# Six base tiles in place of five between the expert products of a two-layer adapter and expert kernel, with the tables and the first products reordered

## The reference

```python
def reference(x, id0, id1, W0, rw0, rb0, A0, B0, W1, base_w, base_b, A1, B1, rw1):
    # layer 0: one of 16 matrices (64 x 64) for each batch, over its tokens; 8 experts of rank 16, the best two
    y = einsum('bct,bcd->bdt', x, W0[id0])
    logits = y @ rw0.T + rb0
    w = gates of the two largest softmax values, normed to 1
    x = x + einsum('no,eor->..', (y @ A0) * w, B0) * 0.5
    # layer 1: one of 14 adapters (1024 x 1024) for each batch; then a base product and 16 experts of rank 64
    y = einsum('bij,bkj->bik', x, W1[id1])
    base = y @ base_w.T + base_b
    hidden = y @ A1.T
    top two of softmax(y @ rw1.T), normed
    return x + base + 0.5 * sum over the two experts of gate * hidden @ B1[e].T
```

## Time and profile before

| | |
|---|---|
| time, 3 runs | 1112.93, 1116.61 (median), 1119.01 us |
| the profiled execution | 1121.12 us, of which its span is 1119.5 us |
| PE busy | 1078.9 us, 96% of the span |
| DVE, ACT, POOL busy | 60%, 45%, 20% |
| granted clock of PE, mean | 0.985 |
| moved by DMA | 283.57 MB, 253 GB/s over the span |

### The profile page before, as it was taken

How to read it: one execution, slowest core, us unless ns; L and a number is a source line. 1 busy time by engine, 2 the same in 40 slices (tenths; PEclk the granted TensorE clock), 3 DMA queues, 4 the chain that set the end, 5 groups by cost and what they waited for, 6 DMA issues and landing times.

```text
span 1119.5 us, 21551 instructions
## 1 busy us (share of the span) xinstructions
PE 1078.9 (96%) x5804; PEld 918.8 (82%) x5805; DVE 673.3 (60%) x1230; ACT 501.0 (45%) x1021; POOL 221.2 (20%) x354
## 2 busy tenths in 40 slices
PE   5999889999999999999999999999999999999998
PEld 5999878888887888888888877877777888888887
DVE  4778743664837557564546688445555376667666
ACT  1121123654737456564536642145555344444444
POOL 1121010110202011110101000155554232222220
PEclk9999989999999999999999999799999999999999
DMA  9588582673957648583666442169999899999996
GB/s 300 192 319 318 209 318 99 229 271 118 340 183 231 245 138 327 192 271 119 235 229 233 94 135 93 60 228 342 351 352 354 335 407 366 336 363 331 319 342 207
DMA packets 126125, 283.57 MB, mean 253 GB/s; under 512 B 28146, under 2 KB 35570, under 8 KB 124146
## 3 DMA queue, kind: packets, MB, share of 16 engines
q1 hardware_dynamic: 96592, 180.59, 45.5%
q0 software_dynamic: 29216, 102.25, 25.9%
q10 hardware_dynamic: 258, 0.01, 0.0%
HBM read 181.50 MB, written 101.29 MB: 253 GB/s over the span
## 4 chain that ended last, share of the span: by engine, by line
PE 80%; DVE 6%; DMA 5%; ACT 3%; issue 3%; SPq 2%; ACTq 0%; POOL 0%; DVEq 0%; another core or an unknown queue 0%; POOLq 0%
PE psum L1550 17%; PE psum L1552 17%; PE psum L1551 17%; PE psum L1561 4%; PE psum L1659 4%; PE psum L1651 3%; PE psum L1782 3%; PE psum L1783 3%; PE psum L1677 2%; PE psum L1679 2%; PE psum L1791 2%; PE psum L1660 2%; ACT w L885 1%; DMA xp<-act_scratch 1%; DMA delta_scratch<-dl 1%
## 5 line engine op out<-in xcount | busy, mean ns | idle before, releaser
L1550 PE MATMUL psum<-base_hi,xp_hi 128*128 128x512 f32 (+3 forms) x520 | 205.6, 395 | 5.6 <-DVE xp_lo L1264 5.5
L1551 PE MATMUL psum<-base_lo,xp_hi 128*128 128x512 f32 (+3 forms) x520 | 199.9, 384 | 0.0
L1552 PE MATMUL psum<-base_hi,xp_lo 128*128 128x512 f32 (+3 forms) x520 | 199.7, 384 | 0.0
L1550 PE MATMUL psum<-w,xp_hi 128*128 128x512 f32 x448 | 181.2, 405 | 0.0
L1552 PE MATMUL psum<-w,xp_lo 128*128 128x512 f32 x448 | 176.9, 395 | 0.0
L1551 PE MATMUL psum<-w,xp_hi 128*128 128x512 f32 x448 | 176.6, 394 | 0.0
L688 POOL DMA_DIRECT2D raw<-w1T x112 | 59.1, 528 | 417.6 <-DVE w L1130 395.3
L1130 DVE TENSOR_TENSOR w<-raw,w 128x1024 fp32r<-128x1024 f32 x112 | 132.1, 1219 | 11.6 <-ACT w L819 8.5
L866 ACT ACTIVATE xp_hi<-xp 128x256 fp32r<-128x256 f32 x124 | 51.1, 416 | 175.6 <-PE psum L1552 153.8
L1550 PEld LDWEIGHTS psum<-base_hi,xp_hi 128*128 128x128 f32 x520 | 98.6, 190 | 30.2 <-issue 6.0
L1264 DVE TENSOR_TENSOR xp_lo<-xp,xp_hi 128x256 fp32r<-128x256 f32 x124 | 51.7, 424 | 112.5 <-ACT xp_hi L866 89.2
(11 more groups left out here) (289 smaller groups left out, 1932.3 us busy)
## 6 DMA issues: line engine op xcount, KB each, us to landing
raw<-w1T POOLq DMA_DIRECT2D x120, 512.0 KB, 6.9
delta_scratch<-dl SPq DMA_DIRECT2D x80, 512.0 KB
xp<-act_scratch SPq DMA_DIRECT2D x74, 256.0 KB, 3.1
act_scratch<-yT SPq DMA_DIRECT2D x72, 256.0 KB, 2.5
act_scratch<-x1g SPq DMA_DIRECT2D x16, 1024.0 KB, 5.1
x1t<-act_scratch SPq DMA_DIRECT2D x64, 256.0 KB
out<-x1t SPq DMA_DIRECT2D x62, 256.0 KB
xg<-xT SPq DMA_DIRECT2D x15, 1024.0 KB, 8.7
```

Of the source, the lines that this page charges most:

```text
L1550: mm(out, a_hi, b_hi, start=start, stop=False, skip_group_check=True)
L1551: mm(out, a_hi, b_lo, start=False, stop=False, skip_group_check=True)
L1552: return mm(out, a_lo, b_hi, start=False, stop=stop, skip_group_check=True)
```

## The change

The change has five parts. MIXED goes from 5 to 6, so KEPT is 14, FAR is 8 and LAST is 18. `tile_of_rows` is made in halves with two `y_low` behind each. The load of `margin` moves on SP from before the first `load_y` to tile 2. `first_z` comes in quarters, and the sums of the table stand elsewhere among PE's first products; POOL reads its first eight ids before it waits for the matrices. DVE's three table reads move from the end of layer 0 to its third step, and `index_read` moves behind the first `hidden_low`.

```diff
-MIXED = 5
+MIXED = 6
...
             sp.dma_start(lg[:, :, :], sides[0:NB, :, 0:E1].rearrange("(t h) c z -> (h c) t z", h=2)
                          ).then_inc(lg_in, 16)
-            sp.dma_start(margin[:, :, :], sides[0:NB, :, E1:E1 + MARGIN].rearrange("(t h) c z -> (h c) t z", h=2)
-                         ).then_inc(margin_in, 16)
...
                     load_y(t + 2)
+                if t == 2:
+                    sp.dma_start(margin[:, :, :], sides[0:NB, :, E1:E1 + MARGIN].rearrange("(t h) c z -> (h c) t z", h=2)
+                                 ).then_inc(margin_in, 16)
...
-            pool.wait_ge(w0_in, 16 * 3)
+            pool.wait_ge(id0_in, 16)
...
+            first_ids = [id_of(b) for b in range(2 * GB)]
+            pool.wait_ge(w0_in, 16 * 2)
...
             index_3()
-            index_read()
             dve.wait_ge(rbias_in, 16)
             gates0(0)
...
                 if n == 0:
+                    index_read()
                     index_4()
...
+                if n == 2:
+                    dve.wait_ge(table_ready, 1)
+                    used = w_used(dve)
+                    total = start_of(dve, used)
+                    one = alone(dve, 0)
                 if n < NS - 2:
                     gates0(n + 1)
...
             add_x(NG - 2, 1)
-            dve.wait_ge(table_ready, 1)
-            used = w_used(dve)
-            total = start_of(dve, used)
-            one = alone(dve, 0)
             add_x(NG - 1, 0)
...
-            def tile_of_rows():
-                rl(tt(hot_a[:, :, :], bcast(iota[:, 0:NX], 1, 2 * NT), bcast(place_f[:, 0, :], 2, NX), ALU.is_equal))
-                for k in range(2):
-                    ks = slice(k * NT, (k + 1) * NT)
-                    tt(hot_a[:, ks, :], hot_a[:, ks, :].bitcast(F32), bcast(tok[:, :], 2, NX), ALU.mult
-                       ).then_inc(hot_a_done, 1)
+            def tile_of_rows(k):
+                ks = slice(k * NT, (k + 1) * NT)
+                rl(tt(hot_a[:, ks, :], bcast(iota[:, 0:NX], 1, NT), bcast(place_f[:, 0, ks], 2, NX), ALU.is_equal))
+                tt(hot_a[:, ks, :], hot_a[:, ks, :].bitcast(F32), bcast(tok[:, :], 2, NX), ALU.mult
+                   ).then_inc(hot_a_done, 1)
...
-            tile_of_rows()
-            for q in range(4):
-                y_low(6, q)
+            for k in range(2):
+                tile_of_rows(k)
+                for q in (2 * k, 2 * k + 1):
+                    y_low(6, q)
...
+            first_z(0)
             index_sums(1)
+            first_z(1)
             index_sums(2)
-            first_z(0)
-            first_z(1)
+            first_z(2)
+            first_z(3)
+            z_of(1, 0)
             index_sums(3)
-            z_of(1, 0)
             y_of(0)
-            index_sums(4)
             z_of(1, 1)
             y_of(1)
             z_of(2, 0)
+            index_sums(4)
             z_of(2, 1)
```

## The result

The changed kernel takes 1124.69 us (median of 14 runs, 1119.56 to 1127.62), the kernel before 1114.49 us in its 14 (1109.17 to 1119.01). The ratio is 1.0083, 95% interval [1.0062, 1.0104]. The forecast of 1114.1 us and its range up to 1119.0 were wrong, and with them the sign. The profiled execution of after took 1124.42 us (span 1122.8), that of before 1121.1, which is above all of its 14 timed runs; so the two traces are 3.3 us apart where the medians are 10.2, and a difference of a few us between them must be checked on other executions.

What follows compares the result with a forecast made beforehand. The prediction took PE, busy 96% of the span, as the bound, plus its waits and low clock. Terms -3.3 - 0.9 + 0 - 0.3 + 2.0 = -2.5 us gave 1114.1 us against the median of 1116.6; range 1107.3 to 1119.

Steps and rivals of the forecast that it cites:

- Last stage, +2.0: Last stage: the same DMA work in a shorter time and one more kept tile add 2.0 us, bounds 0 to +6.6.
- rival 2: Last stage: DMA bounds its first ten stages, costing +6.6 us in place of +2.0; chance 0.17.
- a deficit against 380 GB/s: Last stage: a run of four pairs asks 415 GB/s for 50 us; at 380 it would fall 4.6 us behind.
- the ring: Last stage: the ring of four finishes hides about half of the 4.6 us by which loads fall behind.
- 414 GB/s without a wait: Last stage: the stretch at 902.5 us held 414 GB/s without a wait, taken as evidence against a DMA bound.
- The experts, -0.3: Expert stretch: the sixth tile adds +0.5 us of waits and removes the 0.8 us `dl` wait; net -0.3, bounds -1.5 to +0.8.
- The premise that PE is full in both places: Last stage and experts: a base tile of 10.8 us leaves one and enters the other at the same price.
- The start, -3.3: Kernel start: the gates begin at 22.8 us in place of 26.10, 3.3 us earlier; bounds 2.0 to 3.7.
- The table reads, -0.9: Layer 0: moving the reads saves 1.2 us at its end and adds 0.3 in the third step; net -0.9.
- the -1.2: End of layer 0: without the register reads between two DVE additions, 1.2 us are saved.
- The matrix in halves, 0: Before tile 6: one wait of 2.4 us replaces two of together 2.24, no gain; bounds -2.2 to +0.2.
- Rival 1: Behind tile 6: the low clock doesn't come, 6.7 us faster, 1107.4; chance 0.25 together with idle returning at layer 0's end.

Runs made afterwards that it cites:

- d5: Kernel before plus an unread 0.13 MB load (64 rows) per finish in the last stage, 4.2 MB in all: mean 1127.7 us in 11 runs.
- e5: Kernel before plus an unread load of 128 rows per finish in the last stage, 8.4 MB in all: mean 1122.3 us in 11 runs.
- m4: Kernel before with MIXED = 4: 0.84% slower than the kernel before.
- h5: Kernel before (five tiles) with the late gathers halved to 2 KB rows, so the output differs: ratio 0.998 to the kernel before.
- b5x: Changed kernel with MIXED = 5, table reads back at the end of layer 0, and a fifth x1 buffer: ratio 1.0009 to the kernel before.
- a5: Changed kernel with MIXED = 5, so all its other edits alone: ratio 1.0009 to the kernel before.
- m6: Kernel before with MIXED = 6 and nothing else: ratio 1.0086 to the kernel before.
- hg: Kernel before with MIXED = 6 and the 56 late gathers halved to 2 KB rows, so the output differs: ratio 1.0012 to the kernel before.
- ro: Kernel before with only the three table reads moved from the end of layer 0 to its third step: the reads cost 0.14%.
- a5rb: Changed kernel with MIXED = 5 and the table reads back at the end of layer 0: ratio 0.9972 to the kernel before.

## Why the prediction was wrong, point by point

**Last stage, +2.0: the step that failed.** It had the mechanism (the same transfers in a shorter time, pairs following pairs, kept loads late) and a size far too small. The waits rose by 6.8 us, above the bound of 6.6 that I gave rival 2; and the stage, which was to shrink by 8.8 us (a tile's 10.8 less the 2.0), shrank by 2.1, from 235.7 to 233.6. Two things went into the +2.0: that a deficit against 380 GB/s builds up only in the run of four pairs, and that the ring hides half of it. In the trace the waits come in the first run of three as well (2.33 us at 931.20), and the ring, which starts full, hid none of it that I can see. The row that I trusted against it, 414 GB/s without a wait at 902.5, stood for more than its 12 us, since the stretches beside it in before hold 408 and 399 GB/s and PE waits for nothing to speak of from 890 to 927.5; but from there on before itself has 344 and 378, and that start of the stage can't stand for the hundred microseconds behind it. The share of 0.96 to 1.04 in the first ten stages said that there was no room, and I gave that rival 0.17. The rival's price came true and its picture of one fixed rate did not (d5 against e5).

**The experts, -0.3.** The waits did shrink (xp_lo 2.4 to 1.8 us, dl 0.8 to 0.5), and the stretch grew by 6.6 us against before's own trace, which looked like a gain. It was that trace that stood high, with the first wait of ACT described under m4: five kernels with the same five tiles show 141.2 to 141.8 us, and only the two that share this wait, h5 and b5x, the 144.3 to 145.2 near its 144.7. The row that I read for PE's waits began at 738 us and left out 1.3 us of waiting for `dl` that stands ahead of it, in the expert stretch too, which began at 733.6; a wait of 0.7 us for ACT's half of `dl` at 739.43 was left out as well. Against a5's 141.3 the sixth tile adds 8.6 to 10 us (m6, after). So moving a tile took 9 us in one place and gave 2 to 4 in the other, the last stage's 236.0 less 231.7 to 233.6. That is 4 to 8 us slower; m6's 9.1 us by medians is a little more, and what makes up the rest isn't shown. The premise that PE is full in both places was about right for the sixth tile, and by that premise alone there was nothing to win: from h5 to hg, with less for DMA to move, no gain is left either (+0.3%, which is within the intervals of the two).

**The start, -3.3:** measured -3.05, inside the bounds. Group 1's first half began at 16.55, as worked out, and its 16 records took 2.09 us where the 16 before them took 3.76. Whether that factor is the clock stays open: the granted clock is given as 1.00 for both stretches.

**The table reads, -0.9:** of the other sign. Two steps failed. The reads' price was taken from the 1.17 us that showed at the end of layer 0, and in the third step they take 2.89 us of DVE (2.92 in ro, with nothing else moved); less the cover of 0.9 us this is about the 1.97 us that PE waits. Why they show less at the end is open; with the earlier start, in a5rb, it is 2.10 us there. And the -1.2 didn't come, since behind the reads stood the landing of a store, 1.06 us. In after PE then runs from about 77.0 to 80.4 us at the low clock, in a5 too; in ro, behind the same wait of 2.00 us, the clock stays high. Together this eats the start's gain: a5 1.0009 against a5rb 0.9972.

**The matrix in halves, 0:** one wait of 2.69 us for two of 2.24, as forecast; no run separates it further.

**Rival 1, the low clock that doesn't come,** was not decided by this change. It came in after, m6's profile escaped it and hg's didn't, both with waits of 1.69 and 0.56 to 0.57 us ahead.

## What to carry to other kernels

When work is moved between two stages, ask of each which resource fills it: here the tile's matmuls could move but not its finish's transfers, so that the last stage lost PE work and kept its DMA load. Take the balance from a sweep, as four, five and six tiles here (1.0084, 1 and 1.0086), before believing a sum of local terms: the fifth tile cost the experts some 3 us and the sixth 8 to 10. And a register read costs little where its engine waits anyway; see what else waits there before moving it, and price it where nothing hides it.

## What the hardware showed that I had not expected

The clock behind tile 6 falls in some executions and not in others, and it has a price. The same PE waits precede this stretch of m6 and of hg, which differ in nothing ahead of the last stage; here they are in that order:

```profile
699.00:712.70 13.70, 13.70 (x84) 11.56 (x83) 10.94 (x15) 1.25 (x3) 0.00 (x0) 1.00 0.09 35
```

```profile
699.00:712.70 13.70, 13.70 (x51) 12.05 (x52) 6.41 (x9) 0.83 (x2) 0.00 (x0) 0.57 0.02 7
```

84 matmuls in the one and 51 in the other, so 5 to 6 us. The executions of one kernel part by their mean clock in the same way: on one chip, 11 runs of the kernel before with 0.99 or more average 1111.6 us, 24 below it 1117.5; m6's are 1118.6 and 1127.0. That it is this stretch in each of them was not looked at. So one profiled execution can be 6 us off its kernel's median by the clock alone.

And a transfer's shape can cost more than its bytes: 32 loads of 0.13 MB over 64 rows made a loaded stage 9.9 us longer, 32 of 0.26 MB over 128 rows made it 5.9 longer. Why is open.
